# Attention steps and the seam to the expert tiles: key copies, first-norm statistics and the ranking of two token groups at other places

## The reference

```python
x = x + tanh(g_xattn[0]) * xattn(layernorm(x), ctx, ctx, mask, wq, bq, wk, bk, wv, bv, wo, bo)   # 16 heads of 8
x = x + tanh(g_ffn[0])   * ffn(layernorm(x), router_w, router_b, w1, b1, w2, b2)
# in ffn: top1 = argmax(softmax(x @ router_w + router_b)), and for expert i
h = x @ w1[i] + b1[i]; a, g = split(h, 2)
y = (a * sigmoid(g)) @ w2[i] + b2[i]          # kept where top1 == i
```

## Time and profile before

| | |
|---|---|
| median of 3 executions | 280.25 us (278.69 to 280.58) |
| the profiled execution | 279.12 us, of which the span from first to last instruction is 277.0 us |
| steps -1 to 15 | up to about 148 us of the span |
| expert tiles 0 to 38 | from about 151 us to 267 us |

### The profile page before, as it was taken

The page is one execution under the profiler, slowest core; times in us unless marked ns, Lnnn a source line. Parts: engine busy times, 40 slices in busy tenths (PEclk is TensorE's granted clock), DMA queues, the critical chain, the costliest instruction groups (busy, mean ns, idle before and its releaser), DMA issues.

```text
span 277.0 us, 8574 instructions
## 1 busy us (share of the span) xinstructions
PE 245.9 (89%) x2412; PEld 183.3 (66%) x2412; DVE 220.1 (79%) x641; ACT 156.0 (56%) x435; POOL 153.2 (55%) x254
## 2 busy tenths in 40 slices
PE   1889889999999899999977998989999999999940
PEld 1454434555555455555443998989999999999940
DVE  6968999999989998999976677887787777777720
ACT  4567657778676646554554776555545454444410
POOL 6502455446566448628663586483886455464540
PEclk9999999999999999999988999999999999999995
DMA  7999930000011001102112550263533322100000
GB/s 187 252 309 373 348 101 1 2 4 2 0 41 60 22 23 59 43 2 78 41 62 70 151 163 32 70 196 98 159 95 106 80 78 65 41 23 20 27 0 0
DMA packets 22396, 24.14 MB, mean 87 GB/s; under 512 B 3711, under 2 KB 19522, under 8 KB 22224
## 3 DMA queue, kind: packets, MB, share of 16 engines
q1 hardware_dynamic: 18864, 17.05, 21.5%
q0 software_dynamic: 2784, 6.43, 6.5%
q10 hardware_dynamic: 704, 0.13, 0.3%
HBM read 16.23 MB, written 8.91 MB: 91 GB/s over the span
## 4 chain that ended last, share of the span: by engine, by line
PE 60%; DVE 16%; issue 7%; ACT 5%; POOL 5%; DMA 4%; SPq 1%; POOLq 0%; DVEq 0%; ACTq 0%
PE ps_A L1397 12%; PE ps_B L1397 12%; PE ps_Y L1412 6%; PE ps_O L1412 6%; DVE sb_top L857 5%; PE ps_O L1240 4%; DVE sb_inv L850 3%; ACT sb_pT L614 3%; PE ps_B L1206 2%; PE ps_A L1179 2%; DMA sb_xr<-in_x_dram 2%; POOL routed_rows L412 2%; PE ps_Y L1251 2%; PE ps_B L1270 2%; DVE sb_stats L775 2%
## 5 line engine op out<-in xcount | busy, mean ns | idle before, releaser
L482 POOL DMA_INDIRECT out_dram<-sb_early,sb_k x39 | 41.0, 1052 | 33.2 <-DVE sb_early L1061 27.9
L412 POOL DMA_INDIRECT routed_rows<-sb_xr,sb_pos x32 | 33.2, 1039 | 19.9 <-ACT sb_xr L623 9.1
L857 DVE TENSOR_REDUCE sb_top<-ps_A 128x16 f32<-128x1024 f32 x32 | 38.9, 1217 | 3.8 <-PE ps_A L1184 3.1
L1397 PE MATMUL ps_A<-sb_early 128*128 128x128 f32 x320 | 39.2, 276 | 1.1 <-issue 1.1
L614 ACT ACTIVATE sb_pT<-ps_B 128x512 f32<-128x512 f32 x64 | 33.0, 603 | 9.5 <-PE ps_B L1223 9.5
L1397 PEld LDWEIGHTS ps_A<-sb_early 128*128 128x128 f32 x320 | 37.3, 192 | 1.3 <-issue 1.2
L1397 PE MATMUL ps_B<-sb_early 128*128 128x128 f32 x304 | 37.3, 276 | 0.3 <-issue 0.3
L697 ACT ACTIVATE sb_qT<-ps_A,sb_b1T 128x128 f32<-128x128 f32 x80 | 22.8, 367 | 23.7 <-PE ps_A L1397 23.6
L697 ACT ACTIVATE sb_qT<-ps_B,sb_b1T 128x128 f32<-128x128 f32 x76 | 21.8, 368 | 25.4 <-PE ps_B L1397 25.4
L1397 PEld LDWEIGHTS ps_B<-sb_early 128*128 128x128 f32 x304 | 35.5, 192 | 0.7 <-issue 0.6
L1050 DVE SCALAR_TENSOR_TENSOR sb_qT<-ps_A,sb_b1T,sb_qT 128x128 f32<-128x128 f32 x80 | 22.5, 345 | 13.2 <-ACT sb_qT L697 11.2
(11 more groups left out here) (181 smaller groups left out, 473.0 us busy)
## 6 DMA issues: line engine op xcount, KB each, us to landing
sb_k<-routed_rows SPq DMA_DIRECT2D x39, 132.0 KB, 2.2
sb_w<-in_L_ffn_w_dram SPq DMA_DIRECT2D x4, 1024.0 KB, 11.2
sb_w<-in_L_ffn_w_dram SPq DMA_DIRECT2D x4, 512.0 KB, 10.0
sb_xr<-in_x_dram SPq DMA_DIRECT2D x3, 512.0 KB, 7.3
routed_rows<-routed_rows SPq DMA_DIRECT2D x8, 132.0 KB
routed_rows<-sb_pad_rows SPq DMA_DIRECT2D x7, 132.0 KB, 5.7
out_dram<-sb_early,sb_k POOLq DMA_INDIRECT x39, 2.6
sb_ctx_sb<-in_ctx_dram SPq DMA_DIRECT2D x1, 512.0 KB, 4.7
```

The lines of the kernel that those rows point to most:

```text
L412: pool.indirect_dma_start(routed[:, :], bass.IndirectOffsetOnAxis(ap=pos[:, t:t + 1], axis=0), xr[:, t, :], None, bounds_check=ROWS - 1, o ...
L482: pool.indirect_dma_start(out_rows, bass.IndirectOffsetOnAxis(ap=fr[:, k, 2 * D:2 * D + 1].bitcast(I32), axis=0), fo[:, k, :], None, bound ...
L857: dve.tensor_reduce(top[:, b % 2, t, :], psA[:, :].rearrange("p (h k) -> p h k", k=C), AX.X, ALU.max).then_inc(a_max, 1)
L1397: last = pe.matmul((up_bank, gate_bank)[c](k)[:, f * P:(f + 1) * P], w_1s[:, k, o:o + P], fxT[:, k, :], start=True, stop=True)
```

## The change

Same computation, same instructions but for how the statistics are cut; what differs is the place of some of them.

- ACT: `keys8(1, h)` stands ahead of `norm2(i-1)` and `normalize_rows(i+5)` in its step.
- DVE: the statistics of tiles 16 to 31 leave steps 0 to 3 and are taken in pieces of 4, 3, 3, 2 and 4 tiles at the end of steps 1, 2, 3, 4 and 7. POOL's `rstd(4)` to `rstd(7)` go to steps 2, 4, 5 and 8. The aggregates count on a semaphore of their own.
- Group 3 (step 14): `ranks` on PE goes ahead of `turn2(12)` and the second half of `maxima(15)`, `place` on DVE ahead of the second `maximum`. POOL may send four tiles in step 14 where it sent two, and has no scatters and no wait in step 15.
- Group 4: `choose` goes from the end of step 14 into the seam, `ranks` from step 15 to behind `up(0)` and `turn(1)` (into another bank), and `place` behind `invert(B - 1)`.
- Seam: PE runs `up(0)` directly behind `turn(0)`; ACT loads the sigmoid table first and takes `norm2(B - 2)` ahead of `rows(0)`, and `rows(1)` behind `gates_of(0)`; DVE takes the residual and statistics of batch 14 ahead of the first weight copy. The last two transposes of the second norm wait for group 4's placement.

```diff
+    STATS_AT = {1: (16, 20), 2: (20, 23), 3: (23, 26), 4: (26, 28), 7: (28, 32)}
+    RSTD_AT = {2: 4, 4: 5, 5: 6, 8: 7}
...
-                room = 3 if i in (B - 4, B - 3) else 2
+                room = {B - 4: 3, B - 3: 3, B - 2: 4}.get(i, 2)
...
-                if i == B - 1:
-                    pool.wait_ge(p_ready, G * (B - 1) + 1)
                 while sent < ready and room:
                     scatter(sent)
...
-                if 1 <= i <= 4:
-                    rstd(3 + i)
+                if i in RSTD_AT:
+                    rstd(RSTD_AT[i])
...
+                if 0 <= i < KB - 2:
+                    for h in ((0, 1), (2, 3), (4,), (5,), (6,), (7,))[i]:
+                        keys8(1, h)
                 if has(i - 1):
                     norm2(i - 1)
                 if i >= 0 and streamed(i + 5):
                     normalize_rows(i + 5)
-                if 0 <= i < KB - 2:
-                    for h in ((0, 1), (2, 3), (4,), (5,), (6,), (7,))[i]:
-                        keys8(1, h)
...
             weights(0)
+            act.activation(hold[:, :], tanh_g[0:1, 0:1], ACT.Sigmoid).then_inc(sigmoid_set, 1)
             logits_out(B - 3)
-            act.activation(hold[:, :], tanh_g[0:1, 0:1], ACT.Sigmoid).then_inc(sigmoid_set, 1)
+            norm2(B - 2)
             rows(0)
             weights(1)
-            rows(1)
-            norm2(B - 2)
             act.wait_ge(b1_ready, 1)
             gates_of(0)
+            rows(1)
...
+                if i == place_at[EARLY]:
+                    place(EARLY)
...
-                if 0 <= i < 4:
-                    statistics(4 + i)
-                for n, (b0, b_end) in enumerate(GROUPS):
-                    if choose_at[n] == i and b_end > LATE:
-                        choose(n)
+                if i in STATS_AT:
+                    statistics(*STATS_AT[i])
...
             invert(B - 2)
             first_table()
+            add_residual(B - 2)
+            statistics2(B - 2)
+            moments2(B - 2)
             dve.wait_ge(table1_ready, 2)
             dve.wait_ge(w_big, W_BIG)
             weights(0, expert(0))
+            choose(LAST_GROUP - 1)
             weights(1, expert(1))
-            add_residual(B - 2)
-            statistics2(B - 2)
-            moments2(B - 2)
+            invert(B - 1)
             place(LAST_GROUP - 1)
-            invert(B - 1)
             gate(0)
...
+                if i == place_at[EARLY]:
+                    ranks(EARLY)
                 if has(i - 2):
                     turn2(i - 2)
...
             turn(0)
+            up(0)
             turn(1)
-            up(0)
+            ranks(LAST_GROUP - 1)
             for t in range(FT):
                 if t == 0:
                     output(B - 1)
```

More of the change, by code:

```diff
@@ L764, in _, with statistics @@
             dve.tensor_copy(region_first[:, :], region_int[:, :]).then_inc(const_dve, 1)
-            def statistics(c):
-                t0, t1 = c * SG, (c + 1) * SG
+            def statistics(t0, t1):
                 if t1 <= SPLIT:
@@ L803, in keys8 @@
                                   ALU.mult).then_inc(k8_dve, 1)
-            statistics(0)
+            statistics(0, 4)
             dve.wait_ge(ctx_psum, 2)
@@ L819, in _ @@
             dve.tensor_copy(maskT[:, :], psM16[:, 0:S]).then_inc(mask_evac, 1)
-            statistics(1)
+            statistics(4, 8)
             for h in range(2, H2):
@@ L944, in _ @@
                     output_bias()
-                    statistics(3)
+                    statistics(12, 16)
                 if has(i - 1):
@@ L958, in _ @@
                 for n, (b0, b_end) in enumerate(GROUPS):
-                    if place_at[n] == i:
+                    if place_at[n] == i and n < EARLY:
                         place(n)
@@ L963, in _ @@
                         keys4(0, h)
-                    statistics(2)
+                    statistics(8, 12)
                     for h in range(1, HG):
```

18 lines of the change are left out of this document (10 added, 8 removed).

## The result

The changed kernel takes **276.88 us** (median of 4 executions, 276.11 to 279.0) against 280.15 for the kernel before (4 executions, 278.69 to 280.58). The ratio is 0.9897, with a 95% interval of 0.9856 to 0.9939. Timed again in a later job it took 277.57 (6 executions) against 281.44, ratio 0.9888 (0.9831 to 0.9945). So it is about 1.1% faster, 3 us, and both intervals lie under 1.

What follows compares the result with a forecast made beforehand. PE was taken to bound the expert tiles, with the bound changing from step to step in attention. Attention steps -2.5 and seam -1.1 made -3.6 from 280.25, so 276.65, said as 276.8 us; range 275.3 to 279.8.

Steps and rivals of the forecast that it cites:

- Step 1: Attention step 1: key copies in ACT's idle time and statistics off DVE let step 2 start at 38.55, -2.3 us.
- Step 2: Attention step 2: without DVE's head start it runs at the floor of about 7.4 us, +0.4.
- Steps 3 and 4: Attention steps 3 and 4: fewer statistics on DVE bring both to the floor of 7.4 us, -0.6.
- Steps 5 and 6: Attention steps 5 and 6: the second shift operation, stalled beside POOL's long product, parts from it; step 6 at 8.0, -0.6.
- Steps 7 to 9: Attention steps 7 to 9: 1.24 us of statistics added on DVE cost +0.5, bounds +0.25 to +0.85 by a scatter stall.
- Step 14: Step 14 on PE: the earlier ranks wait for the exponentials ahead of `values(14)`, +0.3 us.
- main case: Full clock in the seam: -3.6 us by the terms, 276.8 us said (275.3 to 277.8), chance 0.45.
- the rival with a fall: PE's clock falls again in the seam: -2.5 + 0.45 = -2.05, 278.2 us, chance 0.28.
- Seam at full clock: Seam: `up(0)` 2.6 us sooner less 1.5 lost by `up(3)`, -1.1; at the lower clock +0.45.
- What takes it back: Behind `up(0)`: late ranks and placement delay `rstd_2(15)` by 1.35 us, ACT's queue adds 0.1 to 0.2, all reaching `up(3)`.
- The rival of the late placement: Seam: `place` of group 4 on DVE holds POOL; `up(3)` +3 against -2.5 in the steps, 280.8 us, chance 0.07.
- the steps give little: Attention steps: PE's floor and DVE leave only about -1.05; 278.1 us at full clock, 279.65 at lower, chance 0.20.

Runs made afterwards that it cites:

- e1: The kernel before with only the key copies moved ahead of the norms on ACT: 278.79 us, ratio 0.995 (0.991 to 1.000).
- e2: The kernel before with only the statistics in pieces and POOL's `rstd` later: 280.01 us, ratio 0.997 (0.993 to 1.000).
- e3: The kernel before with both key copies and statistics moved, seam, steps 14 and 15 and group 4 as before: 278.80 us, ratio 0.996 (0.991 to 1.000).
- e5: The changed kernel, unaltered, timed again in a later job: 277.57 us, ratio 0.989 (0.983 to 0.995).
- e12: The kernel of e11 with three spins in place of ten behind the last logits of the seam: 274.60 us, ratio 0.977 against the kernel before.
- e4: The changed kernel with key copies, statistics and `rstd` back where they were before, leaving the rearranged seam and steps 14 and 15: 281.83 us, ratio 1.004.
- e7: The changed kernel with `rstd_2(B - 1)` ahead of the two late scatters on POOL: 276.56 us, ratio 0.982 against the kernel before.
- e10: The changed kernel with group 3's ranks late, spins in step 15, and DVE's weight copy of tile 2 ahead of batch 15's residual and moments: 275.79 us.
- e11: The kernel of e10 with the second norm of batch 15 behind `rows(3)` on ACT: 273.17 us, ratio 0.975 against the kernel before.

## Why the prediction was right, and where only in sum

The forecast was 276.8; 276.88 was measured. That it is met to a tenth is luck: the median of four lies midway between an execution with no fall (276.19) and one with falls (277.57), and the second timing gave 277.57. The parts:

- **Step 1, -2.3**: -2.36, and the two savings are worth 1.24 and 1.18 singly (e1, e2). **Step 2, +0.4**: +0.41. The working by ACT's idle time held: the norm is at 36.55 (36.5 said).
- **Steps 3 and 4, -0.6**: -0.34. They stop at 7.62 and 7.45; in step 3 PE is busy for 7.33 and DVE for 7.26, and it does not reach 7.4. **Steps 5 and 6, -0.6**: -0.30, by the named stall.
- **Steps 7 to 9, +0.5**: -0.56. This term had the wrong sign. Steps 7 and 8 are 7.45 and 7.66 as before (the four tiles fitted: DVE busy 6.39 of 7.45), and step 9 fell from 8.68 to 8.12. At the end of step 8 DVE now has no stall, so it enters step 9 sooner. All kernels with the new statistics (after, e2, e3, e5 to e12) show 8.12 or 8.13 there, and those with the old (e1, e4) 8.68; the keys have no part in it. I had written that this stall "may get better or not" and yet bounded the term at +0.25: the lower bound had to be negative.
- **Steps 10 to 13, nothing**: +0.78, of which 0.22 in step 11 and 0.55 in step 12. It is in e4 as well, whose steps are those of before, and in e1; the profile of before happened to miss the collision in part. Against e4's steps the gain is 110.29 - 107.19 = 3.1, against the profile of before 2.35 (2.5 said).
- **Step 14, +0.3**: the wait is 0.44. What was not foreseen is the fall of the clock *there*. The prediction looked for a fall in the seam only. Its main case, the clock staying up, had a chance of 0.45; of the ten executions of this kernel two have a mean clock of 0.988, and eight have falls. So the rival with a fall (278.2, chance 0.28) is closer to what most executions do, with the fall often at another place.
- **The last scatter 1.9 sooner**: 1.88. `first_table` was hidden, though two of its small operations took 0.77 and 0.63 us, one beside the last scatter and one beside the bias addition behind it.
- **`up(0)`**: at full clock 149.6 was said, 149.6 - 133.26 = 16.3 behind step 14; e4 shows 16.13. With one fall, meant in the seam, 151.15, so 17.9; e5, whose one fall is in step 14, shows 17.75. With both, 19.39 in the profiled execution. Seam at full clock -1.1, measured -1.30; with one fall +0.45, measured 17.75 + 10.10 - 27.52 = +0.33.
- **What takes it back, 1.35 to 1.55**: 10.10 - 8.59 = 1.51, with `rstd_2(15)` 6.29 behind `up(0)` (6.1 said) and `up(3)` behind ACT. Size and way are right, the cause is not complete: the late scatters on POOL can go without any gain (e7), DVE is as late, waiting for the same late ranks, and DVE's weight copy holds `up(2)` as well (e10).

Two of the prediction's own signs of being wrong came true: step 14 got longer, and DVE and POOL collide otherwise in steps 8 to 12. A third thing it looked for, step 8 or 9 longer than before, did not come: step 9 is shorter.

So the number is right because errors cancel: the steps gave a little less in the profile, and the clock case is a mixture. Executions of the changed kernel at clock 0.988 take 276.1 to 276.2, those with falls 275.8 to 279.2. The rival of the late placement as a new bound had the right place, but its price is 1.5 and not 3. That the steps give little (-1.05) is refuted by the traces: step 14 starts 2.3 us sooner in the changed kernel and in every other one with both parts of the steps (e3, e5 to e12). The median of e3 alone would not decide it.

For the clock the prediction weighed a rule of the Trainium skill (TensorE: Matmul & The Clock Gate, Part 1: The HAM clock gate), by which half speed follows on PE being idle for a whole stretch. The rows after do not agree with it either: between 132.00 and 134.00 PE was busy for 1.56 of 2.00 us, and the clock fell.

## What to carry to other kernels

Ask of a step that is moved ahead what its result is waited for by: the ranks of group 3 came sooner, POOL could not take them before 136.3 anyway, and PE paid with a wait and, in more executions, with the clock. Leave work in PE's queue where its input is surely there, and let the waits fall on engines with room. A wait that you take away may have hidden another cost: the old seam absorbed a fall of the clock, the new one pays for it (e1, e4). Where one wait ends last by a tenth, look for the second behind it before undoing the first (e10, e11), and where spins cover a wait for a transfer, cutting them wins nothing (e12). Judge a kernel whose clock falls in some executions by the granted clock of each, not by one profile.
